# Sort of layer two in a two-layer graph network: the place one-hots carry the code, column by column

## What is computed

```python
h = jnp.maximum(_layernorm(x, axis=-1), 0.0)
neigh = jax.ops.segment_sum(h[src], dst, num_segments=N_NODES)
x = x + relu(relu(((1.0 + eps[0]) * h + neigh) @ W1 + b1) @ W2 + b2)
h = jnp.maximum(_layernorm(x, axis=-1), 0.0)
weights = jnp.einsum('rb,bio->rio', coefficients, bases)
out = h @ w_self.T
out = out.at[src].add(sum over r of where(edge_type == r, h[dst] @ weights[r], 0))
x = x + out
```

## Time and profile before

| | |
|---|---|
| median of 3 runs | 1506.08 us (1504.79 to 1512.66) |
| profiled execution | 1494.55 us, span 1492.7 us |
| granted PE clock, mean of the span | 0.757 |
| PE busy | 903.5 us (61%) |
| DVE busy | 732.0 us (49%) |
| POOL busy | 824.6 us (55%) |
| ACT busy | 399.1 us (27%) |

### The profile page before, as it was taken

One profiled execution on the slowest core, in us unless ns is written; L12 is line 12 of the kernel. 1 busy time (PEld: TensorE's weight loads), 2 busy tenths in 40 slices (PEclk: granted clock), 3 DMA queues, 4 the chain that ended last, 5 costly groups with the idle time before them and its releaser, 6 DMA issues.

```text
span 1492.7 us, 13816 instructions
## 1 busy us (share of the span) xinstructions
PE 903.5 (61%) x4119; PEld 565.2 (38%) x4119; DVE 732.0 (49%) x2202; ACT 399.1 (27%) x943; POOL 824.6 (55%) x833
## 2 busy tenths in 40 slices
PE   2731962387780068899978835946657445456554
PEld 2610530154450045576654412524435223333333
DVE  6740985275687596799965401313333212222222
ACT  6310840154450055688743302200000000000000
POOL 0176627576517447666660372066766667666762
PEclk9665885698895579899997966966767566665766
DMA  3432313234322123333332834711111111111113
GB/s 82 128 81 71 101 55 104 61 95 119 81 67 79 48 70 95 85 118 113 110 74 62 254 93 131 249 50 43 50 42 47 46 48 47 48 46 44 48 45 65
DMA packets 50239, 122.92 MB, mean 82 GB/s; under 512 B 16084, under 2 KB 26949, under 8 KB 47415
## 3 DMA queue, kind: packets, MB, share of 16 engines
q0 software_dynamic: 33088, 67.82, 17.8%
q1 hardware_dynamic: 16772, 52.61, 11.2%
q10 hardware_dynamic: 308, 1.60, 0.4%
HBM read 71.86 MB, written 50.10 MB: 82 GB/s over the span
## 4 chain that ended last, share of the span: by engine, by line
PE 23%; DVE 16%; another core or an unknown queue 10%; POOL 10%; issue 10%; DMA 1%; ACT 0%; DVEq 0%; POOLq 0%; ACTq 0%
PE ps L904 11%; POOL gathered L412 10%; PE ps L988 5%; DVE scratch L710 4%; DVE node_hot L736 3%; PE ps L885 2%; PE ps L887 2%; PE ps L908 2%; DVE spare L662 2%; DVE place_val_a L705 1%; DVE place_hot L700 1%; DVE spare L612 1%; DVE chunk_f L667 1%; DMA gathered<-z_table,row_of 1%
## 5 line engine op out<-in xcount | busy, mean ns | idle before, releaser
L412 POOL DMA_INDIRECT gathered<-h_table,row_of x416 | 432.4, 1039 | 346.1 <-issue 116.2
L412 POOL DMA_INDIRECT gathered<-z_table,row_of x410 | 389.6, 950 | 298.9 <-issue 117.1
L904 PE MATMUL ps<-node_hot,gathered 128*128 128x250 f32 x820 | 280.4, 495 | 233.4 <-issue 140.8
L478 ACT ACTIVATE place_val_b<-place_hot,code_b 125x128 f16<-125x128 f16 x728 | 315.1, 517 | 389.2 <-DVE place_hot L700 302.3
L736 DVE TENSOR_SCALAR node_hot<-iota_f,key_of 128x250 f32<-128x250 f32 x410 | 141.2, 377 | 376.1 <-PE ps L904 172.5
L908 PE MATMUL ps<-node_hot,gathered 128*128 128x506 bf16 (+1 forms) x1248 | 246.3, 344 | 123.0 <-DVE node_hot L736 64.1
L904 PEld LDWEIGHTS ps<-node_hot,gathered 128*128 128x128 f32 x820 | 187.7, 246 | 325.8 <-issue 304.4
L885 PE MATMUL ps<-scratch,place_val_a 125*128 125x410 f16 (+2 forms) x728 | 204.3, 311 | 55.2 <-issue 27.7
L887 PE MATMUL ps<-scratch,place_val_b 125*128 125x410 f16 (+2 forms) x728 | 201.6, 306 | 30.5 <-issue 29.3
L908 PEld LDWEIGHTS ps<-node_hot,gathered 128*128 128x128 bf16 x1248 | 124.1, 102 | 224.3 <-issue 158.7
L710 DVE TENSOR_SCALAR scratch<-iota_h,chunk_f 125x410 f16<-125x410 f16 (+2 forms) x728 | 163.4, 304 | 5.9 <-issue 1.4
(11 more groups left out here) (152 smaller groups left out, 393.9 us busy)
## 6 DMA issues: line engine op xcount, KB each, us to landing
z_table<-spare SPq DMA_DIRECT2D x50, 448.0 KB
z_table<-zeros_z SPq DMA_DIRECT2D x19, 896.0 KB
gathered<-h_table,row_of POOLq DMA_INDIRECT x416
gathered<-z_table,row_of POOLq DMA_INDIRECT x410
z_table<-spare SPq DMA_DIRECT2D x50, 52.0 KB
z_table<-zeros_z SPq DMA_DIRECT2D x19, 104.0 KB
out<-x_sb SPq DMA_DIRECT2D x6, 224.0 KB
h_table<-gathered SPq DMA_DIRECT2D x1, 1092.0 KB
```

Of the source, the lines that this page charges most:

```text
L412: pool.indirect_dma_start(place if s == LAST else place.rearrange("p j d -> p (j d)"), None, z_table if s == LAST else h_table, bass.Indir ...
L478: nc.scalar.activation(place_val_b[:, buf, i, :], place_hot[:, buf, :, i], ACT.Copy, scale=code_b[l][:, c0 + batch * BATCH + i:c0 + batch ...
L904: last = T.matmul(psf[:, bass.ds(offs[i], WIDE[s])], rows, node_hot_of[s][:, k % HOTS[s], :], start=False, stop=False, skip_group_check=True)
```

## The change

It touches the last sort (s = 3) alone. In `sort_batch`'s place stands `sort_last`: DVE makes the place one-hot with the high code in it for one column at a time, `(iota == place) * code`, one operation with one tensor input and two scalars per partition, written contiguously (`place_code_a`, in the memory of `place_val_a`). `place_hot` is not made. ACT waits for each column (`code_ready`) and scales it to the low part, for which `code_b` becomes the ratio of the low code to the high code; so that the high code is never zero, it is counted up by one from 2048 on, and `read_last` takes that off again after the sort. The place and the high code are kept as fp32 in the memory of `src_i` and `dst_i`.

```diff
+        place_code_a = place_val_a[:, :, :, :].rearrange("p u v b -> p u (v b)").rearrange("p u (b v) -> p u b v", b=BATCH)
+        place_f, code_f1 = src_i.bitcast(F32), dst_i.bitcast(F32)
...
-            for s in range(1, NSORT):
+            for s in range(1, LAST):
                 batches_alone(s, sort_batch, 0, COLS[s] // BATCH)
+
+            def sort_last(batch, buf):
+
+                for i in range(BATCH):
+                    act.wait_ge(code_ready, batch * BATCH + i + 1)
+                    nc.scalar.activation(place_val_b[:, buf, i, :], place_code_a[:, buf, i, :], ACT.Copy,
+                                         scale=code_b[1][:, batch * BATCH + i:batch * BATCH + i + 1]).then_inc(val_ready, 1)
...
-                own(V.tensor_copy(place_h[l][:, cs], scr1))
+                own(V.tensor_copy(place_f[:, :] if s == LAST else place_h[l][:, cs], scr1))
...
+                if s == LAST:
+                    own(V.tensor_scalar(code_f1[:, :], scr0, HALF_CODE, None, ALU.is_ge))
+                    own(V.scalar_tensor_tensor(code_f1[:, :], scr0, -HALF_CODE, code_f1[:, :], ALU.add, ALU.add))
+                    own(V.tensor_scalar(scr1.bitcast(F32), scr1, -HALF_CODE, 1.0 / CODE, ALU.add, ALU.mult))
+                    own(V.reciprocal(code_b[1][:, :], code_f1[:, :]))
+                    own(V.tensor_tensor(code_b[1][:, :], code_b[1][:, :], scr1.bitcast(F32), ALU.mult))
+                    return
                 V.tensor_scalar(code_a[l][:, cs], scr0, -HALF_CODE, None, ALU.add)
...
+            def sort_last(s, batch, buf):
+
+                dve.wait_ge(batch_used, batch + (BATCHES_BEFORE[s] + 1))
+                for i in range(BATCH):
+                    c = batch * BATCH + i
+                    V.tensor_scalar(place_code_a[:, buf, i, :], iota_h[0:EP, 0:P], place_f[:, c:c + 1], code_f1[:, c:c + 1],
+                                    ALU.is_equal, ALU.mult).then_inc(code_ready, 1)
+                for i in range(BATCH):
+                    c = batch * BATCH + i
+                    last = V.tensor_scalar(chunk_hot[:, buf, i, 0:CHUNKS[s]], iota_h[0:EP, 0:CHUNKS[s]],
+                                           chunk_f[1][:, c:c + 1], None, ALU.is_equal)
+                last.then_inc(batch_ready, 1)
+
+            def read_last():
+
+                w = CHUNKS[LAST]
+                above, value = (scratch[:, i * WIDEST:i * WIDEST + w] for i in (1, 2))
+                dve.wait_ge(batch_used, BATCH_BUFS + BATCHES_BEFORE[LAST] + COLS[LAST] // BATCH)
+                own(V.tensor_scalar(above, ps[:, 7, 0:w], 0.25, None, ALU.is_ge))
+                own(V.scalar_tensor_tensor(value, ps[:, 7, 0:w], 0.0, above, ALU.add, ALU.subtract))
+                V.tensor_scalar(s0[:, 0:w], value, HALF_CODE + 0.5, CODE, ALU.add, ALU.mult).then_inc(sorted_read, 1)
+                dve.wait_ge(sorted_read, LAST + 1)
...
-                groups_beside(s - 1, node_hots, sort_batch)
-                read_sorted(s)
+                groups_beside(s - 1, node_hots, sort_last if s == LAST else sort_batch)
+                if s == LAST:
+                    read_last()
+                else:
+                    read_sorted(s)
...
-                    T.matmul(ps[:, 7, 0:w], place_val_a[:, buf, :, i], hot, start=False, stop=False, skip_group_check=True)
+                    T.matmul(ps[:, 7, 0:w], place_code_a[:, buf, i, :] if s == LAST else place_val_a[:, buf, :, i], hot, start=False, stop=False, skip_group_check=True)
```

4 lines of the change are left out of this document (3 added, 1 removed).

## The result

The changed kernel takes 1522.06 us (median of nine runs, 1509.04 to 1535.78) against 1503.58 us for the kernel before in nine runs beside it: ratio 1.0119, 95% interval 1.0090 to 1.0147, so slower by 1.2%, some 18 us. The profiled execution took 1517.65 us (span 1515.8) against 1494.55 (span 1492.7) before. The time forecast was 1522.3. The sizes of the operations came out as forecast; the way in which they add up did not, and most of the experiments are about that.

What follows compares the result with a forecast made beforehand. VectorE was taken to bound the sort's rounds, 4.12 us against TensorE's 4.08. Placing +4.1, heads +11.1 and reading +1.0 sum to +16.2 us, added to the 1506.08 us median: 1522.3 us, likeliest case 1515 to 1533, wider range 1503 to 1534.

Steps and rivals of the forecast that it cites:

- The reciprocal: Placing of layer two's edges: a new reciprocal over 400 columns, 2.74 us (2.77 with the wait), within placing's +4.1 us.
- The eight operations: Head of a sort batch: eight two-scalar operations, 0.224 us each, 1.79 us in place of 1.44, +0.35 a round.
- second scalar free: Rival, head of a batch: the second scalar costs nothing, head 1.31 us, total 1506.9 us, no change; chance 0.27.
- slower form: Rival, head of a batch: the operation fits no fast form, 0.29 us each, +34 us, 1540 us; chance 0.05.
- small operations at 0.09 us: Rival, head of a batch: eight operations take about 0.8 us, TensorE bounds, 1505.2 us, no change; chance 0.05.
- TensorE's 4.08 us a round: Sort rounds: 16 sort matmuls in 2.80 us and 12 summing matmuls in 1.28, the bound if VectorE gets faster.
- Reading: Reading of the sorted row: three operations in place of one, +1.0 us, all on the path.
- worth nothing in a quiet round: Sort rounds: ScalarE's gain by contiguous input is worth nothing, since it stands behind VectorE.
- the batches before 625 us I cost at nothing: Early part of the last sort: VectorE's idle time covers the longer head's +0.35 us a round, so 0 us.
- the 33 behind them: Sort batches from 625.11 to 760.44 us: VectorE bounds, each loses 0.35 us, +11.6 less some 0.5, +11.1 us.
- some 0.5 by which TensorE is behind at 625 us: Sort at 625 us: taken off the +11.6 us of the 33 batches, leaving +11.1 us.
- The last 0.05 of the chances: Chance 0.05 of a gain over 0.5% by something unseen, needing TensorE's stalls before 625 us to shrink.

Runs made afterwards that it cites:

- e1: c0 with one of the two scalars of each place operation an immediate (the high code left out): 1514.4 us, ratio 1.0101.
- e5: c0 with both scalars of each place operation immediates (place and high code left out): 1499.8 us, ratio 0.9947.
- e4: c0 with ScalarE and TensorE reading their columns every eighth element again, as before the change: 1533.1 us, ratio 1.0206.
- c0: Control: the changed kernel, but layer two gathers a fixed list of rows in place of the sorted ones: 1525.1 us, ratio 1.0131.
- e6: The changed kernel with a one-column memset on GpSimd behind every gather of the third sort: 1518.9 us, ratio 1.0089.
- e8: The kernel before with a POOL break (two memsets of 410 columns and a wait) behind every fourth gather of the third sort: 1483.3 us, ratio 0.9895.
- e9: The changed kernel with the same POOL break as e8 behind every fourth gather of the third sort: 1511.7 us, ratio 1.0066.
- e3: The changed kernel with VectorE waiting on its own last operation ahead of the chunk one-hots and of the node one-hots: 1519.2 us, ratio 1.0094.
- e11: The kernel before, POOL waiting after every second gather until it has landed, in all three sorts' gathers of layer one: 1714.5 us, ratio 1.1405.
- e10: The kernel before, POOL waiting after every second gather until it has landed, in the third sort alone: 1611.0 us, ratio 1.0739.

## Why the prediction was right, and where not

**Right in its steps on VectorE.** The reciprocal was forecast at 2.74 us from the slope of two small rows and took 2.65. "VectorE: DVE Perf Modes" of the Trainium skill (8-slice pipeline), by which it was an estimated 3.5 us, was further off. The eight operations are 0.224 us apart, as forecast from 0.104 with no scalar and 0.164 with one; e1 and e5 show the row of prices once more, from rounds of VectorE of 4.46, 3.98 and some 3.5 to 3.75 us. The first and the third rival (second scalar free, slower form) are out by this, and so is the second, small operations at 0.09 us. TensorE's 4.08 us a round is not its least, though the rivals take it for that: in e1 rounds of 3.98 us follow each other. Reading cost +1.04, forecast +1.0. ScalarE became faster (388 ns an activation instead of 517) and is busy 21.90 of the 40 us from 640 to 680, so it waits for L739: worth nothing in a quiet round, as forecast, though its worth for the total stayed open in e4.

**Wrong in "the batches before 625 us I cost at nothing: VectorE's idle time there covers +0.35", and in the 33 behind them.** The sum had 0 us up to the eighteenth head and +11.1 from there to the last; the profiles have -13.1 and +34.7, and c0 and e6 bear out both parts. The first step took the idle time for something fixed, that belongs to the stretch. It belongs to POOL: TensorE's stalls there come with gathers issued back to back (T4). In the changed kernel most of these gathers are held, POOL is seldom back to back, most of those stalls go, and the early rounds run for the most part at VectorE's 4.46 us, which is still less than before with its stalls. The second step took the later rounds for quiet ones that lose 0.35 each. They do, 32 x 0.34 = 10.9 us, but some 24 us of stalls come on top, which were not there before. Over the whole way early gain and late loss cancel but for a few us: what is lost is 34 us against 29, no more than single profiles differ by, and what is left is VectorE's longer round, 49 x 0.34 = 16.7 us, which the pair e8 and e9 shows as 16.1. How many stalls come, and where, differs from one kernel to the next (e1 and e4, with held gathers, lose 60 and 59 us), and no run here foretells it.

**Not foreseen: POOL.** The prediction treats POOL as touched by the reading alone. That VectorE's new round, without an operation on two tensors or a wait in it, would hold one of POOL's gathers for 1.95 us in each quiet round was in no step and no rival.

**Why the time still agrees.** The steps gave +16.2 us on the profiled execution, 1510.8, and it took 1517.65. The medians stand 18.5 us apart, nearer to the steps than the two profiles, and the median of three runs to which the sum was added, 1506.08, lay 2.5 us above that of nine. So the agreement to 0.3 us is luck, and so is that of the steps: two parts that were off by 13 and 24 us went opposite ways. The sign and the sizes on VectorE are not luck. The sum also takes off "some 0.5 by which TensorE is behind at 625 us", for which no row is shown; it is too small to matter here. The last 0.05 of the chances was kept for a gain "which would need the stalls of TensorE before 625 us to shrink": they did shrink, by 13 us and more, and later stalls took it back.

## What to carry to other kernels

Idle time that covers an added cost is a cover only if you know whose it is: find out what makes it, and whether your change moves that. An operation on VectorE is not only its duration: a run of small operations without a wait can hold POOL's gathers, so look at POOL's mean times for each stage after every change on VectorE. An engine that issues gathers without a break can slow the others instruction by instruction, which shows as waits on "issue" 0.7 us apart and 1.4 us in a chain of one engine, and no dependency names it. And compare a stage in parts, against two profiles or more of each kernel: a total that comes out as forecast can hide a gain and a loss.

## What the runs showed of the hardware

- A gather of POOL takes 0.95 us undisturbed, 2.90 when it starts with VectorE's run of L743 and L779 (2.7 us without a wait), and 0.95 on the mean where two waits stand in VectorE's round (e3). The other way round a chunk one-hot of 0.32 us took 1.74 beside POOL's two memsets (e8). This fits "SBUF — State Buffer" of the Trainium skill (two separate sides), which says that VectorE's and GpSimd's shared pair of ports is a lock held for a whole instruction, and that descriptors written by GpSimd are held up by it. The rows show more: the gather is held over many short operations in a row, and not always. In the changed kernel the held ones start from 0.59 us before the start of L743 to 0.21 us behind it, but for one at 0.91; those that start 0.54 to 0.60 us behind it pass through the same run in 0.95 us (618.38 us), while in c0 some that start 0.62 to 0.91 us behind are held for 1.96 to 2.24 us. So the rows give no clean rule, and why is open.
- With POOL at a cycle of 1.25 to 1.4 us, single instructions on TensorE and VectorE come 0.7 us apart; twenty operations with a wait each took 26.7 us instead of 13.36. Breaks of POOL end it (e8, e11, the first part of e10, and in before the end of the filling at 507.84 us). A count of gathers that starts it is not shown: TensorE's stalls began 12 gathers behind the last break or held one in the changed kernel (715 us) and 6 in c0 (564 us), while in before VectorE's chain in the ranking slowed down only at 476 us, 28 gathers behind POOL's last break. What in the chip carries it was not tried; the packets of the instruction queues that the trace shows are too few to tell.
- The same signs stand in layer two, which no experiment touched: before, TensorE's summing there (L904) has 140.8 us of waits on "issue" while POOL gathers from the z table. Whether breaks of POOL would shorten it was not tried.
- A wait of VectorE for its own last operation cost 0.11 us behind the place operations and 0.14 behind the chunk one-hots (e3, rounds of 4.74 us instead of 4.46), not the 0.06 to 0.1 that was expected.
